# Cross-attention over a masked context: keys in five pieces of 400 instead of four of 416

## The reference

```python
query, key_, value = proj(q, w_q), proj(k, w_k), proj(v, w_v)     # 16 heads of 32
scores = einsum('bhqd,bhkd->bhqk', query, key_) / sqrt(32)
scores = where(mask == 0, -1e9, scores)
out = einsum('bhqk,bhkd->bhqd', softmax(scores), value) @ w_o.T
x = x + out
# then self-attention with LoRA on q and v, then a mixture of 20 experts, top 2
```

## Time and profile before

| | us |
|---|---|
| median of 3 runs | 839.92 |
| lowest and highest | 837.32, 842.08 |
| the profiled execution | 836.71 |
| its span, first to last instruction | 834.8 |
| TensorE busy | 730.8 (88%) |
| VectorE, ScalarE, GpSimd busy | 407.4, 360.9, 309.4 |

### The profile page before, as it was taken

How to read it: one execution, slowest core, us unless ns; L and a number is a source line. 1 busy time by engine, 2 the same in 40 slices (tenths; PEclk the granted TensorE clock), 3 DMA queues, 4 the chain that set the end, 5 groups by cost and what they waited for, 6 DMA issues and landing times.

```text
span 834.8 us, 16882 instructions
## 1 busy us (share of the span) xinstructions
PE 730.8 (88%) x6819; PEld 590.2 (71%) x6819; DVE 407.4 (49%) x835; ACT 360.9 (43%) x640; POOL 309.4 (37%) x250
## 2 busy tenths in 40 slices
PE   1999999899999999999999999998877626998980
PEld 0888778777888778887788778887665412776660
DVE  5814442354344442444434355335674472587755
ACT  2434551564344543545334435223354310687860
POOL 0005532552355523664245526002233036243334
PEclk9999999999999999999999999999898755899995
DMA  9201499220021100111010020100000855499948
GB/s 309 98 0 43 107 257 165 92 92 27 17 93 43 42 14 30 42 43 42 5 39 2 2 68 2 63 22 33 2 2 2 326 215 199 153 368 419 404 135 311
DMA packets 43655, 90.34 MB, mean 108 GB/s; under 512 B 7370, under 2 KB 26186, under 8 KB 39086
## 3 DMA queue, kind: packets, MB, share of 16 engines
q1 hardware_dynamic: 40126, 77.83, 28.4%
q0 software_dynamic: 3440, 11.31, 3.4%
HBM read 66.55 MB, written 22.65 MB: 107 GB/s over the span
## 4 chain that ended last, share of the span: by engine, by line
PE 69%; DMA 8%; DVE 8%; issue 7%; SPq 5%; ACT 2%; POOL 1%; DVEq 0%; POOLq 0%; ACTq 0%
PE bank L177 18%; PE bank L178 17%; PE bank L179 17%; PE bank L183 8%; SPq L1725 4%; PE bank L332 3%; DMA xi<-scratch_xg 3%; PE bank L309 3%; DMA scratch_ys<-xm,xi 2%; DMA craw<-in_ctx 2%; DVE x_sb L1540 1%; DMA scratch_ys<-hT,xi 1%; PE bank L538 1%; DVE stats L1288 1%; DVE xu L1034 1%
## 5 line engine op out<-in xcount | busy, mean ns | idle before, releaser
L1568 POOL TENSOR_SCALAR pp<-pp,rl 128x416 f32<-128x416 f32 x128 | 193.2, 1529 | 223.0 <-DVE rl L1130 223.0
L1219 DVE CUSTOM_DVE_ANT_0 pp<-bank,cap 128x416 f32<-128x416 f32 x128 | 68.8, 585 | 63.9 <-PE bank L309 63.9
L177 PE MATMUL bank<-chi,wk 128*128 128x416 f32 x256 | 95.6, 373 | 0.0
L1186 DVE COPY pt<-bank 128x512 f32<-128x512 f32 x64 | 44.2, 691 | 104.5 <-PE bank L183 104.5
L803 ACT ACTIVATE pp<-pp,acc 128x416 f32<-128x416 f32 x128 | 80.7, 633 | 31.1 <-DVE acc L1219 31.1
L179 PE MATMUL bank<-chi,wk 128*128 128x416 f32 x256 | 90.4, 353 | 0.0
L178 PE MATMUL bank<-clo,wk 128*128 128x416 f32 x256 | 90.4, 353 | 0.0
L177 PE MATMUL bank<-wv,chi 128*128 128x512 f32 x208 | 86.2, 415 | 2.7 <-issue 2.7
L178 PE MATMUL bank<-wv,chi 128*128 128x512 f32 x208 | 81.3, 391 | 0.0
L179 PE MATMUL bank<-wv,clo 128*128 128x512 f32 x208 | 81.1, 390 | 0.0
L177 PE MATMUL bank<-wh,xu 128*128 128x512 f32 x152 | 66.4, 437 | 7.6 <-DVE xu L1034 3.2
(11 more groups left out here) (226 smaller groups left out, 1392.2 us busy)
## 6 DMA issues: line engine op xcount, KB each, us to landing
wr<-in_We SPq DMA_DIRECT2D x19, 1024.0 KB, 8.8
craw<-in_ctx SPq DMA_DIRECT2D x16, 832.0 KB, 4.6
scratch_xg<-zero SPq DMA_DIRECT2D x20, 448.0 KB, 7.8
raw<-in_We SPq DMA_DIRECT2D x8, 1024.0 KB, 8.9
xi<-scratch_xg SPq DMA_DIRECT2D x28, 258.0 KB
wr<-scratch_ys SPq DMA_DIRECT2D x8, 512.0 KB, 6.7
x_sb<-in_x SPq DMA_DIRECT2D x2, 1024.0 KB, 9.9
out_dram<-x_sb SPq DMA_DIRECT2D x8, 256.0 KB, 4.7
```

Of the source, the lines that this page charges most:

```text
L177: pe.matmul(o, lhs[0], rhs[0], start=start, stop=False)
L1186: dve.tensor_copy(pt[:, p8 % 4, :, :].rearrange("p a c -> p (a c)"), at("t", 8 * (n - 1) + p8)[:, :]).then_inc(S["v_pt"], 1)
L1219: dve.tensor_tensor_reduce(out=frame(p8), in0=scores[:, p8 % 4, :], in1=cap[:, :], scale=-1.0, scalar=nm[:, b, p8:p8 + 1] if seg else 3e38 ...
L1568: pool.tensor_scalar(frame(p8), frame(p8), rl[:, n % 2, p8:p8 + 1], None, ALU.mult).then_inc(S["g_pn"], 1)
```

## The change

There are five pieces of 400 keys, with 399 made-up keys ahead of the first. Eight batches of a piece are 3200 keys, exactly 25 tiles of 128: four tiles are made in batch 0 and 8, and three in every other one. Seven of the 25 tiles hold keys of two batches (before, three of 13). The copy ahead of the left half is now made in batches 1, 3 and 5 of eight, with 32, 64 and 96 columns. Windows of `pp` move by 16 columns from batch to batch, in a frame with 112 zero columns. Tables and searches for the pieces have five places. The other layers are untouched.

```diff
-    NB, D, T, CW, PW, NC_, E, X8 = 16, 512, 1024, 416, 96, 4, 20, 15
+    NB, D, T, CW, PW, NC_, E, X8 = 16, 512, 1024, 400, 112, 5, 20, 15
-    LAST = E + X8
+    LAST, LEAD = E + X8, 96
...
-        chi = sb("chi", [128, 4, 64 + 2 * CW], f32r, lasting)
-        clo = sb("clo", [128, 4, 64 + 2 * CW], f32r, lasting)
+        chi = sb("chi", [128, 4, LEAD + 2 * CW], f32r, lasting)
+        clo = sb("clo", [128, 4, LEAD + 2 * CW], f32r, lasting)
...
-            return 13 * (n // 4) + (0, 4, 7, 10)[n % 4]
+            return 25 * (n // 8) + (0, 4, 7, 10, 13, 16, 19, 22)[n % 8]
+
+        def shared(n):
+
+            return CW * (n % 8 + 1) % 128
 
         def tile_columns(v, k, j):
 
-            c = 64 + 128 * j if j < 6 else 128 * j - 768
+            m, at_key = divmod(128 * j, CW)
+            c = LEAD + CW * (m % 2) + at_key if m % 2 == 0 or at_key + 128 <= CW else LEAD + at_key - CW
             return v[:, k, c:c + 128]
...
-            f, m = D * p8 + PW, n % 4
-            c = f + (0, -32, -64, -96)[m] + 128 * i4
+            c = D * p8 + PW - CW * (n % 8) % 128 + 128 * i4
             return pp[:, c:c + 128]
...
-                if j % 13 in (3, 6, 9):
+                if j % 25 % 3 == 0 and j % 25 not in (0, 24):
                     pe.wait_ge(S["v_ctx"], n + 2)
...
-                if n % 4 == 1:
-                    copy(chi[:, :, 0:64], craw[:, :, CW - 64:CW])
+                if n % 2 and shared(n):
+                    copy(chi[:, :, LEAD - shared(n):LEAD], craw[:, :, CW - shared(n):CW])
...
-            own.on(dve.tensor_tensor(frow[:, 8:12], frow[:, 0:4], cst[0:1, 136:140], ALU.mult))
+            own.on(dve.tensor_tensor(frow[:, 10:15], frow[:, 0:5], cst[0:1, 142:147], ALU.mult))
...
-                if n % 4 == 1:
-                    rest(clo[:, :, 0:64], craw[:, :, CW - 64:CW], chi[:, :, 0:64])
+                if n % 2 and shared(n):
+                    ahead = slice(LEAD - shared(n), LEAD)
+                    rest(clo[:, :, ahead], craw[:, :, CW - shared(n):CW], chi[:, :, ahead])
...
-    NC, CW, K = 4, 416, 1601
+    NC, CW, K = 5, 400, 1601
```

More of the change, by code:

```diff
@@ L77, in perceiver @@
         first = ExitStack()
-        cm = sb("cm", [128, 4], f32, first)
+        cm = sb("cm", [128, NC_], f32, first)
         fl = sb("fl", [128, 16], f32, first)
         rows = sb("rows", [128, 4], f32, first)
-        fr = sb("fr", [4, 1], f32, first)
+        fr = sb("fr", [NC_, 1], f32, first)
         frow = sb("frow", [1, 32], f32, first)
@@ L249, in tensor @@
             pe.wait_ge(S["v_ids"], 1)
-            pe.transpose(pb[7][0:4, 0:128], fl[:, 0:4], ident).then_inc(S["p_ids"], 1)
+            pe.transpose(pb[7][0:NC_, 0:128], fl[:, 0:NC_], ident).then_inc(S["p_ids"], 1)
             pe.wait_ge(S["v_ids"], 2)
-            pe.matmul(pb[7][0:1, 0:8], fr[:, :], cst[0:4, 128:136], start=True, stop=True).then_inc(S["p_ids"], 1)
+            pe.matmul(pb[7][0:1, 0:10], fr[:, :], cst[0:NC_, 128:138], start=True, stop=True).then_inc(S["p_ids"], 1)
             def turn_x(i):
@@ L288, in v_part @@
                 for k in range(4):
-                    last = mm3(pe, at("v", j)[:, :], [tile_columns(c, k, j % 13) for c in (chi, clo)],
+                    last = mm3(pe, at("v", j)[:, :], [tile_columns(c, k, j % 25) for c in (chi, clo)],
                                [w[:, k, :] for w in wv], k == 0, k == 3)
@@ L1062, in vector @@
             dve.wait_ge(own.sem, own.n)
-            dve.tensor_scalar(fl[:, 0:4], cm[:, :], rows[:, 2:3], None, ALU.max).then_inc(S["v_ids"], 1)
+            dve.tensor_scalar(fl[:, 0:NC_], cm[:, :], rows[:, 2:3], None, ALU.max).then_inc(S["v_ids"], 1)
             dve.wait_ge(d_x[0], 16)
@@ L1066, in vector @@
             dve.wait_ge(S["p_ids"], 1)
[L1067 removed]
+            dve.tensor_reduce(fr[:, :], pb[7][0:NC_, 0:128], AX.X, ALU.max).then_inc(S["v_ids"], 1)
             own.on(bn(1))
             dve.wait_ge(S["p_ids"], 2)
[L1070 removed]
+            dve.tensor_copy(frow[:, 0:10], pb[7][0:1, 0:10]).then_inc(S["v_ids"], 1)
             dve.wait_ge(S["v_ids"], 3)
             dve.wait_ge(S["d_cst"], 16)
[L1073 removed]
+            own.on(dve.tensor_tensor(frow[:, 10:15], frow[:, 0:5], cst[0:1, 142:147], ALU.mult))
             for j in range(NC_):
                 dve.wait_ge(own.sem, own.n)
[L1076 to L1078 removed]
+                own.on(dve.scalar_tensor_tensor(out=frow[:, 15:20], in0=frow[:, 5:10], scalar=float(j + 1),
+                                                in1=frow[:, 10:15], op0=ALU.is_equal, op1=ALU.mult,
+                                                accum_out=frow[:, 20 + j:21 + j]))
             dve.wait_ge(own.sem, own.n)
[L1080 to L1081 removed]
+            dve.tensor_copy(ids[:, 0:5], frow[:, 20:25]).then_inc(S["v_ids"], 1)
+            dve.tensor_copy(ids[:, 5:6], frow[:, 9:10]).then_inc(S["v_ids"], 1)
             def scaled(i, n):
@@ L1883 @@
     cst[:, 0:128] = _np.eye(128)
-    cst[0:4, 128:132] = _np.eye(4)
-    cst[0:4, 132:136] = _np.triu(_np.ones((4, 4)))
-    cst[0, 136:140] = _np.arange(4)
+    cst[0:5, 128:133] = _np.eye(5)
+    cst[0:5, 133:138] = _np.triu(_np.ones((5, 5)))
+    cst[0, 142:147] = _np.arange(5)
     cst[:, 140] = -0.5
```

23 lines of the change are left out of this document (9 added, 14 removed).

## The result

The changed kernel is faster. Over ten executions each, run side by side, the median is 830.38 us (826.04 to 835.21) after and 837.25 us (835.96 to 842.08) before; the ratio is 0.9928, with a 95% interval of 0.9904 to 0.9951. That is a gain of 6.0 us, between 4 and 8 (the two medians lie 6.9 apart). The forecast was 832.2 us and 7.7 us of gain. The profiled execution took 833.81 us with a span of 832.0, so it is one of the slower ones; a second profile of the same kernel (the first experiment) has a span of 829.0.

A forecast was written before the change was run, and what follows sets the result against it. TensorE was taken as the bound (69% of the chain, 99.34 of 100 us busy mid-cross-attention). Savings of 11.7 us less 1.4, 1.3 and 1.25 gave 7.7 off the 839.9 median: 832.2 us, range 827.5 to 838.5.

The forecast's parts named there:

- Values, -5.5: Cross-attention value tiles: 52 become 50, batches 4 and 12 having three instead of four, 2.75 us each; saves 5.5 us.
- Keys, -5.2: 768 key matmuls lose 16 columns each, 0.43 ns a column, 6.8 ns a matmul; saves 5.2 us.
- Scores, -1.0: 32 halves of the scores shorten with their columns; saves 1.0 us, between nothing and 1.1.
- Start, +1.4: Before the first projection: larger mask reduction 0.38, search step 0.19, mask landing 0.8; costs 1.4 us (0.6 to 1.7).
- Waits for the next context, +1.3: Third value tiles waiting for VectorE's split of the next batch's context, twelve batches instead of eight; costs 1.3 us (0.7 to 2.2).
- Batch 3, +1.25: Third value tile waits for batch 4's context, queued behind stores of zeros; pause 4.9 us; costs 1.25 us (0.5 to 3.0).
- the prediction's own last sentence: Signs of being wrong: transposes over 0.1 us apart in even batches, 188 ns between key matmuls, low clock over 3.4 us near 155.
- the keys don't follow their columns: Rival: something else, such as weight loads, sets 188 ns between key matmuls; all 5.2 us missing, 837.4 us; 8%.
- transposes load slower from new places: Rival: weight windows at odd multiples of 16 columns slow 256 transposes in even batches; twice as long gives 850 us; 5%.
- the holes cost more: Rival: second low-clock stretch near batch 3 (+1.7), start and waits at upper ends (+0.3, +0.9); 835.1 us; 14%.
- they cost nothing new: Rival: start and waits add nothing, the mask being hidden by other transfers; 830 us; 8%.
- The second piece: Rival: a second piece of keys opens, costing another 16 batches, over 380 us; chance none.

The follow-up runs named there:

- the first experiment: The changed kernel run and traced again, unaltered: median 830.13 us, ratio 0.9929 to the kernel before.
- the experiment that adds two: The changed kernel with the third value tile of batches 4 and 12 computed twice: median 837.0 us, ratio 1.0001 to the kernel before.
- the table: Trace comparison of the kernels before and after, both with stores of zeros spread over batches 3 to 7: cross-attention 423.9 and 415.9 us.
- the gap: The changed kernel with an unused 32-column tile ahead of `craw`, shifting it and all behind by 128 bytes: median 828.74 us, ratio 0.9905 to the kernel before.
- 384 columns: The changed kernel with key matmuls of 384 instead of 400 columns, last 16 keys left out: median 828.2 us, ratio 0.9897 to the kernel before.
- the smaller mask: The changed kernel loading and reducing only the last four mask pieces, 1600 of 2000 columns: median 828.29 us, ratio 0.9895 to the kernel before.
- spread stores: Both kernels with the 20 stores of zeros in five lots behind context loads of batches 3 to 7: after 824.04 us (0.9867), before 831.42 (0.9959).
- the early split: Both kernels with stores spread and VectorE's split of the next context ahead of the four maxima: after 819.43 us (0.9807), before 829.43 (0.9914).

## Why the prediction was right, point by point

The forecast of 832.2 lies 1.8 us above the measured median, and the direction and the main terms hold. It forecast more gain than was measured and still lies above the result, because it took its 7.7 us off the median of three executions, 839.92, and that of ten is 837.25. Step by step:

**Values, -5.5.** Right: 2.83 us a tile, 2.82 in the experiment that adds two. But the other 50 tiles did not stay as they were: 24 of them now begin where matmuls are slower by 3 to 4 ns. That takes back 1.0 us, and the table has -4.7. No step of the prediction had this term.

**Keys, -5.2.** The mechanism is right (time goes with columns), the size a little off: 183.4 ns and not 181 behind 188.9 in the mean, so 5.6 ns a matmul where 6.8 were forecast, 768 x 5.6 = 4.3 us. In the cross-attention, which has 60 of the 64 groups, it is 4.0. The missing 0.9 is again a matter of place. The prediction read its 188 from the keys of batch 6, an even batch; the odd ones, whose columns begin 416 further on (1664 bytes, an odd multiple of 128), had more before the change already, 189 to 190, as the keys of batch 5 show:

```profile
187.19 0.35 PE L178 MATMUL bank<-clo,wk 128*128 128x416 f32 x1
...
189.08 0.35 PE L179 MATMUL bank<-chi,wk 128*128 128x416 f32 x1
```

Over the whole kernel before, even batches have 188.0 ns and odd ones 189.8. After the change both have 183.4, and with the gap both have 180 to 181. If these are the faster places, it is 7.6 ns from one to the other, where 6.8 were forecast; that they are is argued and not shown. The Trainium skill's page "TensorE: Matmul & The Clock Gate" (Back-to-back issue gap) would have given 1.6 us by its sustained figures; the traces of this case (188, 183 and 176 ns at 416, 400 and 384 columns) do not agree with them.

**Scores, -1.0.** 0.02 to 0.03 us a half, 32 halves: 0.6 to 1.0. At the lower edge of what was taken.

**Start, +1.4.** The term that was mis-sized most. The reduction (2.24 - 1.89 = 0.35) and the search step (0.19) are as forecast. The landing of the mask is not: it came at 7.9 to 8.2 us in three traces with four pieces and at 9.5 to 10.0 in eight with five, 1.7 later on the mean, where 0.8 was taken and 1.1 was the upper bound. That bound was the wrong step: it scaled the 5.3 us of the transfer by its bytes, but the profile's line has 7.0 us for 500 KB, a third more time for a fifth more bytes. Bytes explain the step from 400 to 500 KB (5.8 to 7.0); what else the cut into pieces of 400 costs is open, as said at the smaller mask. The first projection starts at 25.0 to 25.3 before and at 27.1 to 27.6 after, 2.2 us later. Another 0.6 us comes from the query projection's 96 matmuls, at 233.3 ns and not 227.5. Most of that is their place in memory, as 229.2 with the gap shows.

**Waits for the next context, +1.3.** Right in mechanism and near in size, with one batch left out of the sum. Batch 4, forecast at 0.75, in TensorE's timeline:

```profile
180.15 0.93 PE L313 MATMUL bank<-kk,qc 32*64 32x400 f32 x16
181.73 0.47 PE L177 MATMUL bank<-wv,chi 128*128 128x512 f32 x1 [0.66 <-issue]
...
184.58 1.03 PE L183 MATMUL bank<-cst,pp 128*128 128x128 f32 x8
185.37 0.43 PE L177 MATMUL bank<-chi,wk 128*128 128x400 f32 x1
```

VectorE there, copy ahead and split of batch 5 merged:

```profile
179.35 2.27 DVE L1038 TENSOR_TENSOR clo<-craw,chi 128x384 fp32r<-128x384 f32 x2
```

Batch 10, forecast at 0.63, TensorE (its scores start at 335.01):

```profile
336.51 0.47 PE L177 MATMUL bank<-wv,chi 128*128 128x512 f32 x1 [0.57 <-issue]
```

And VectorE there:

```profile
334.27 2.14 DVE L1038 TENSOR_TENSOR clo<-craw,chi 128x256 fp32r<-128x256 f32 x2
```

Batches 4 and 12 wait 1.58 - 0.86 = 0.72 us, batches 2 and 10 wait 0.64, batches 1, 5, 9 and 13 wait 0.26 and batches 6, 11 and 14 wait 0.30, for 0.29 forecast. The eleven besides batch 3 come to 4.7 us, where the eight before had 3.2: +1.5. The prediction names batch 2 among those that waited before but has no term for it after; it has the place of batch 10, and with its +0.23 the prediction's own sum would have been 1.6.

**Batch 3, +1.25.** Right in place and size: 0.9 to 1.3 by the two traces of after. In its parts it went another way. The pause was 5.65 us, not 4.9, and the low clock lasted 6.8 us, not 3.4. By the prediction's own last sentence that is a mark against it, and the step that it hits is where the low clock falls: the forecast counted 3.4 us of it, all under work, and it came in the pause already. The cost is near the forecast even so, 1.4 us and not 1.7 in the first trace, because only 3 of the 6.8 us fell on work; in the second trace it was 2.2, with a wait 1.0 shorter. That the two parts trade against each other so that the sum hardly moves was not foreseen, and that it came to 1.25 is in part luck.

**The sum.** Keys 4.3, values 4.7 and scores 0.8, less 2.8 for the start (2.2 and 0.6), 1.5 for the waits and 1.1 for batch 3: 4.4 us. The ratio gives 6.0, with an interval of 4 to 8, in which the sum lies. The stretches of the two traces stand nearer to the sum (TensorE's first value matmul 3.2 us later, the cross-attention 6.8 shorter: 3.6 us). The other two pairs lean the same way: with spread stores the stretches give 2.6 and -8.0, 5.4 us, the ratios 7.7; with the early split 2.1 and -9.7, 7.6 us, the ratios 9. Each time 1.4 to 2.4 us of the measured gain have no place in the traces. None of the three differences is clear of noise by much (the first pair's 3.6 lies just outside its interval, the other two lie inside theirs), but all lean the same way. The stretch behind the cross-attention, where the code does not differ, took 341.3 to 346.2 us in three traces with pieces of 416 and 342.6 to 346.9 in nine with 400, which is no gain and too scattered to exclude one. This stays open. The forecast of 7.7 came so near partly by luck: by the traces it was too high, by 3 us against the sum of rows, for the dearer start and the places in memory, and the times then gave back a part that nobody has found.

**The rivals.** That the keys don't follow their columns fell with 183 ns, and finally with 176 at 384 columns. That transposes load slower from new places fell with 0.79 us for eight in batch 4, an even batch. That the holes cost more was right for the start (2.2 to 2.8 against an upper end of 1.7) and wrong for the clock. That they cost nothing new fell with all of these rows. The second piece did not open: 256 key matmuls.

## What to carry to other kernels

Where TensorE is busy 99% of a stretch, a column less is worth its streaming time, and this can be read from the spacing of matmul starts at two widths, with the operands at like places in memory. What has to be looked for is who waits anew: a tile that moves over the border of two batches inherits the whole delay of the next batch's load, and by the stretches of the traces the change gained 7.6 us and not 3.6 (by the ratios 9 and not 6) once neither a queue of stores nor VectorE's order held that load and its split back. A larger input at the head of the program, whose answer everyone waits for, should be priced by its measured landing and with a wide upper bound, not by its bytes alone.

## What the runs showed of the hardware

The place of operands in memory: 128 bytes of shift swap which value tiles have 229 and which 232 to 233 ns between matmuls of 512 columns, where only the weights moved, and take 3 ns off each key matmul and 4 off each of the query projection, where only the streamed operand moved. So either operand's place counts. The kernel before shows it without any shift: its key matmuls have 188.0 ns in even batches and 189.8 in odd ones, whose start lies an odd multiple of 128 bytes further. It fits that operands are slower whose start lies in the second half of a stretch of 256 bytes; but that rests on sums of tile sizes, and one shift was tried, so the rule is argued and only the effect is shown. In this kernel it is worth 1.6 us of cross-attention, less than the times tell apart.

The low clock costs only what is left of it when work comes back. In the kernel after it fell inside TensorE's pause and lasted 6.8 us in both traces: with 3 us of it under work it cost some 1.4 us in the value tile (4.24 us from 154.47 to 158.71, where batch 4's takes 2.85), with 4.6 under work 2.2. In the kernel before it fell at 154.1, when TensorE had begun again at 152.40, and all of its 3.4 us were under work.
